# Layer 0's cross attention: scores and band mask over four quadrants, moved ahead of the attended values, with the residual between the two units on VectorE

## The chip, the core and the metric

The kernel runs on one core of one Trainium2 chip. The metric is the device time of one execution in microseconds (us); the result of a version is the median over its runs. The engines are TensorE (PE in the rows; PEld are its weight loads), VectorE (DVE), ScalarE (ACT), GpSimd (POOL) and SyncE (SP). Each engine works through its own instruction queue in order; engines wait for each other by semaphores.

## The reference, cut to what matters

The program is a decoder of two layers. After each sublayer the input is added back and normalised. Only the second sublayer, the cross attention of layer 0, is touched:

```python
q = heads(query @ Wq.T + bq)      # 32 sequences of 128 tokens, D = 256, H = 16 heads of HD = 16
k = heads(key @ Wk.T + bk)        # key = value = the context, 32 x 128 x 256
v = heads(value @ Wv.T + bv)
scores = einsum('bhqd,bhkd->bhqk', q, k) / sqrt(16)
local  = abs(i[:, None] - i[None, :]) <= 64            # a band: 128 queries x 128 keys
attn   = softmax(where(local, scores, -inf), axis=-1)
ctx    = einsum('bhqk,bhkd->bhqd', attn, v)
x      = layernorm(x + (ctx.reshape(B, S, 256) @ Wo.T + bo))
```

## The kernel before

`l0_xattn` handles one sequence of 128 tokens as one tile: 32 tiles, numbered `n`, in 8 groups of 4. The 16 heads of a tile are two units `u` of 8 heads. In a unit, `q` picks a half of the unit and `c` a half of the model dimension; the four combinations (`u`, `q`) are four quarters of 32 partitions of the projected queries and keys, and each quarter's scores have a PSUM bank of their own.

A list called `walk` sets the order on every engine: for step `s` it calls each entry `(lag, count, f)` as `f(s - lag)`. So the entries' order is the order of the engine's queue inside a step, and the lag says which tile is handled. Before the change, step `s` holds:

* **TensorE**: `score(s)` (matmuls of 32 rows, line 973, then the band mask as matmuls of a 64-row identity with `bandb`, line 978; once for each unit), `transpose_e(s-2)` (four blocks `j` of four transposes, line 992; blocks 0 and 1 are unit 0, blocks 2 and 3 are unit 1), one part of the projections of a group to come (a group's four parts, `transposes`, `project_q`, `project_k`, `project_v`, lines 934 to 959, fall on four steps in a row, and the last group's on steps 24 to 27), `apply(s-2)` (attended values, line 1001), `multiply(s-3)` (output projection, line 1013).
* **VectorE**: `shift(s)` for both units (maximum, line 1091, and subtraction, line 1094), `sums(s-1)` (row sums, line 1099, and reciprocal `ri`, line 1102), `bias_v` once in a group (line 1110), `residual(s-3)` (lines 1119 to 1126).
* **GpSimd**: `scale_e(s-1)`, which multiplies the exponentials of both units by `ri` (line 882), and at some steps `bias_x` or `roots`.
* **ScalarE**: `copy_et(s-2)` (line 1060), a part's bias or copy, `exponentials(s)` (line 1054), `copy_ot(s-2)` (line 1065), `normalise(s-8)`.

The waits that matter here: `shift` waits for `scored`; `scale_e(n)` waits for `inverted`, which `sums(n)` raises; `transpose_e(n)` waits for `e_scaled`, which `scale_e(n)` raises once for each unit; `residual(n)` waits for `multiplied`. A scored unit's bank is written again once `shifted` says that it was read.

The band mask is made ahead of step 0: GpSimd cuts it (lines 859 to 865), ScalarE copies it to bf16 (line 1027) before it copies the first transposed inputs (`copy_xt`, line 1033). No score is computed before it is there.

Of the kernel before, what the change touches and what calls it, by code (L numbers as in the profile page):

```python
# [8 lines left out]
BF16 = mybir.dt.bfloat16  # L9
I32 = mybir.dt.int32  # L10
U32 = mybir.dt.uint32
ALU = mybir.AluOpType
ACT = mybir.ActivationFunctionType
AX = mybir.AxisListType

P = 128
# [33 lines left out]
def item_done(eng, sem, n, inc=1):  # L50

    eng.wait_ge(sem, (n + 1) * inc)
# [722 lines left out]
def l0_xattn(nc, x_in, ctx4, bv, bo, ah, kv, x_out):  # L775
# [4 lines left out]
    with ExitStack() as stack:  # L780
        kit = Kit(nc, stack, "l0x")
        ident, identb = ah.ident, ah.identb
        band = kit.sb("band", [P, 4, P])
        bandb = kit.sb("bandb", [P, 4, P], BF16)
        w_q, w_k, w_v, w_o = ah.l0_w
        b_q, b_k, par = ah.l0_b_q, ah.l0_b_k, ah.l0_par
        b_v, b_o = kit.sb("b_v", [P, D]), kit.sb("b_o", [P, D])
# [68 lines left out]
        with nc.Block() as block:  # L856
            @block.gpsimd
            def _(pool):
                pool.memset(band[:, :, :], 0.0).then_inc(band_set, 1)
                pool.wait_ge(band_set, 1)  # L860

                pool.affine_select(out=band[:, :, :], in_=band[:, :, :], compare_op=ALU.is_ge, fill=-1e30, base=64,
                                   pattern=[[0, 4], [-1, P]], channel_multiplier=1).then_inc(band_cut, 1)
                pool.wait_ge(band_cut, 1)
                pool.affine_select(out=band[:, :, :], in_=band[:, :, :], compare_op=ALU.is_ge, fill=-1e30, base=64,
                                   pattern=[[0, 4], [1, P]], channel_multiplier=-1).then_inc(band_cut, 1)
                pool.memset(half[:, :], -0.5).then_inc(set_, 1)
                pool.memset(neg[:, :], -1.0).then_inc(set_, 1)
                pool.memset(eps[:, :], LN_EPS).then_inc(set_, 1)
                pool.wait_ge(set_, 3)  # L870
                pool.wait_ge(biases_loaded, 2 * 16)

                def bias_x(g):
                    x_ready(pool, g)
                    slot_free(pool, residual_done, g, 2, G)
                    pool.tensor_tensor(xb[:, g % 2, :, :], x_group(g), b_o[:, :].unsqueeze(1).to_broadcast([P, G, D]),
                                       ALU.add).then_inc(x_biased, 1)

                def scale_e(n):
                    item_done(pool, inverted, n)  # L880
                    for u in range(2):
                        pool.tensor_tensor(e[:, n % 2, u, :, :], e[:, n % 2, u, :, :], spread(ri[:, n % 2, u, :], P),  # L882
                                           ALU.mult).then_inc(e_scaled, 1)
                count = [0]

                def roots(g):
                    item_done(pool, mv_done, g, G)
                    slot_free(pool, normed, g, 2, G)
                    pool.tensor_tensor(ln[:, g % 2, 2, :], mv[:, g % 2, :, 1], eps[:, :], ALU.add).then_inc(ln_step, 1)
                    pool.wait_ge(ln_step, 3 * g + 1)  # L890
                    pool.tensor_tensor(ln[:, g % 2, 0, :], ln[:, g % 2, 2, :], half[:, :], ALU.pow).then_inc(ln_step, 1)
                    pool.wait_ge(ln_step, 3 * g + 2)
                    pool.tensor_tensor(ln[:, g % 2, 3, :], mv[:, g % 2, :, 0], ln[:, g % 2, 0, :], ALU.mult).then_inc(ln_step, 1)
                    pool.wait_ge(ln_step, 3 * g + 3)
                    pool.tensor_tensor(ln[:, g % 2, 1, :], ln[:, g % 2, 3, :], neg[:, :], ALU.mult).then_inc(ln_done, 1)
                walk([(1, TILES, scale_e), at_part(5, bias_x), (G + 3, TILES, lambda n: roots(n // G) if n % G == 0 else None)])
# [31 lines left out]
            def _(pe):  # L928
# [34 lines left out]
                def score(n):  # L963
                    g, t = n // G, n % G
                    if n == 0:
                        pe.wait_ge(band_ready, 1)
                    item_done(pe, k_biased, g, 4)
                    for u in range(2):
                        slot_free(pe, shifted, 2 * n + u, 2)
                        for c in range(2):  # L970
                            for q in range(2):
                                at = slice(32 * (2 * u + q), 32 * (2 * u + q) + 32)
                                pe.matmul(ps_s[u][:, q, 2 * c:2 * c + 2, :], qt[at, g % 2, c, t * P:(t + 1) * P],
                                          kt[at, g % 2, c, :, t * P:(t + 1) * P], start=c == 0, stop=False)
                        for q in range(2):
                            for lo in range(2):
                                rows64, keys64 = slice(64 * lo, 64 * lo + 64), slice(64 - 64 * lo, 128 - 64 * lo)
                                last = pe.matmul(ps_s[u][rows64, q, :, keys64], identb[rows64, rows64], bandb[rows64, :, keys64],
                                                 start=False, stop=True)
                        last.then_inc(scored, 1)  # L980

                def transpose_e(n):
                    for j in range(4):
                        item_done(pe, e_scaled, 2 * n + j // 2)
                        if j == 0:
                            slot_free(pe, ot_copied, n, 1)
                        elif j == 1:
                            slot_free(pe, residual_done, n, 2)
                        else:
                            pe.wait_ge(et_copied, 4 * n + j - 1)  # L990
                        for i in range(4):
                            last = pe.transpose(ps_e[j % 2][:, i, :], e[:, n % 2, j // 2, 4 * (j % 2) + i, :], ident[:, :])  # L992
                        last.then_inc(e_transposed, 1)
# [23 lines left out]
                def early(n):  # L1017
                    if n == 0:
                        pe.wait_ge(v_biased, TILES)
                    kv.make(pe, n, n + 1)  # L1020
                walk([(0, TILES, score), (2, TILES, transpose_e), at_part(0, transposes), at_part(1, project_q), at_part(2, project_k),
                      at_part(3, project_v), (2, TILES, apply), (3, TILES, multiply), (TILES + 1, L0X_LAST, early)])

            @block.scalar
            def _(act):
                act.wait_ge(band_cut, 2)
                act.activation(bandb[:, :, :], band[:, :, :], ACT.Copy).then_inc(band_ready, 1)

                def copy_xt(g):
# [17 lines left out]
                            act.activation(kt[:, g % 2, c, odd, :], ps_p[c][:, :], ACT.Identity, bias=b_kp[:, odd, c:c + 1],  # L1047
                                           scale=par[:, odd:odd + 1]).then_inc(k_biased, 1)

                def exponentials(n):  # L1050
                    slot_free(act, e_transposed, n, 2, 4)
                    for u in range(2):
                        item_done(act, shifted, 2 * n + u)
                        act.activation(e[:, n % 2, u, :, :], sx[:, u, :, :], ACT.Exp, scale=HD ** -0.5).then_inc(exped, 1)

                def copy_et(n):
                    slot_free(act, applied, n, 1)
                    for j in range(4):
                        item_done(act, e_transposed, 4 * n + j)
                        act.activation(et[:, j, :, :], ps_e[j % 2][:, :, :], ACT.Copy).then_inc(et_copied, 1)  # L1060

# [5 lines left out]
                def normalise(n):  # L1067
# [2 lines left out]
                    slot_free(act, stored[g % 2], g // 2, 1, 16)  # L1070
                    act.activation(y[:, g % 2, t, :], r[:, g % 2, t, :], ACT.Identity, scale=ln[:, g % 2, 0, t:t + 1],
                                   bias=ln[:, g % 2, 1, t:t + 1]).then_inc(normed, 1)
                walk([(2, TILES, copy_et), at_part(0, copy_xt), at_part(1, bias_q), at_part(2, bias_k), (0, TILES, exponentials),
                      (2, TILES, copy_ot), (8, TILES, normalise), (TILES + 1, 2, lambda n: kv.keep(act, n, n + 1)),
                      (TILES + 5, L0X_LAST - 2, lambda n: kv.keep(act, n + 2, n + 3))])

            @block.vector
            def _(dve):
# [3 lines left out]
                    ins = dve.tensor_scalar(b_kp[:, odd, :], b_k[:, :], par[:, odd:odd + 1], None, ALU.mult)  # L1082
                ins.then_inc(bkp_done, 1)

                def shift(n):
                    for u in range(2):
                        i = 2 * n + u
                        item_done(dve, scored, i)
                        scores = ps_s[u][:, :, :, :].rearrange("p q h k -> p (q h) k")
                        slot_free(dve, shifted, i, 2)  # L1090
                        dve.tensor_reduce(top[:, u, :], scores, AX.X, ALU.max).then_inc(maxed, 1)
                        item_done(dve, maxed, i)
                        slot_free(dve, exped, i, 2)
                        dve.tensor_tensor(sx[:, u, :, :], scores, spread(top[:, u, :], P), ALU.subtract).then_inc(shifted, 1)

                def sums(n):
                    item_done(dve, exped, n, 2)
# [16 lines left out]
                def residual(n):  # L1114
# [9 lines left out]
                    item_done(dve, stats_done, n)  # L1124
                    slot_free(dve, ln_done, g, 2)
                    dve.bn_aggr(mv[:, g % 2, t, :], stats[:, n % 2, :]).then_inc(mv_done, 1)
                walk([(0, TILES, shift), (1, TILES, sums), at_part(3, bias_v), (3, TILES, residual)])
        kit.clear_semaphores()

# [1856 lines left out]
```

## Time and profile before

| what | value |
|---|---|
| median of 3 runs | 2455.33 us (2452.11 to 2456.83) |
| the profiled execution | 2453.8 us, span 2452.1 us |
| granted TensorE clock over the span | 0.971 |
| busy share of the span: PE, DVE, ACT, POOL | 92%, 55%, 45%, 35% |
| the stage that is changed | from about 446 to 800 us of the span |

### The profile page before, as it was taken

To read this page: it belongs to the slowest core of one execution; us is meant where nothing else is said; L and a number is where in the kernel's file an instruction comes from. 1 tells how busy PE (TensorE), PEld (TensorE's weight loads), DVE (VectorE), ACT (ScalarE), POOL (GpSimd) and SP (SyncE) were. 2 spreads that over 40 slices of the span, in tenths; PEclk is the share of its full clock that TensorE was granted. 3 is DMA by queue.
4 is the path that set the end of the run, shared out by engine and by line. 5 is a ranking of instruction groups with operands and counts; after the bars stand their busy time and mean duration, and the time that the engine had idled before them with its cause. 6 is when DMAs were issued, how large, how long until landed. Compare 5 with 4: busy or idle time off the path is not lost. (4 is left out here: it accounts for less than half of the span.)

```text
span 2452.1 us, 44501 instructions
## 1 busy us (share of the span) xinstructions
PE 2262.6 (92%) x17122; PEld 1768.8 (72%) x17122; DVE 1347.3 (55%) x2517; ACT 1100.5 (45%) x1872; POOL 849.8 (35%) x873
## 2 busy tenths in 40 slices
PE   7999998799998899999999799999995999999993
PEld 5777776466666566757776688888884888888893
DVE  6888888488887680015545567888885111111113
ACT  3666666456565564543334255555552111111113
POOL 3555454244444582000101234455444122222221
PEclk8999999899999999999999899999997999999997
DMA  5435554100110679480211323333332856666665
GB/s 144 113 90 129 137 128 115 61 27 27 53 53 19 214 254 295 149 262 4 69 50 37 112 90 106 104 104 109 104 121 76 293 174 191 193 174 183 194 203 148
DMA packets 204609, 313.21 MB, mean 128 GB/s; under 512 B 63473, under 2 KB 183153, under 8 KB 191089
## 3 DMA queue, kind: packets, MB, share of 16 engines
q1 hardware_dynamic: 184336, 255.25, 33.6%
q0 software_dynamic: 13440, 17.90, 4.1%
q10 hardware_dynamic: 6624, 37.23, 3.9%
q8 instruction: 138, 2.26, 0.4%
q14 instruction: 71, 0.57, 0.1%
HBM read 188.88 MB, written 121.45 MB: 127 GB/s over the span
## 5 line engine op out<-in xcount | busy, mean ns | idle before, releaser
L2748 ACT ACTIVATE dec_area<-me_ps_h 128x512 f32<-128x512 f32 (+1 forms) x160 | 88.7, 554 | 423.8 <-PE me_ps_h L2726 423.8
L2789 DVE TENSOR_SCALAR me_yo<-me_ps_y,moe_xg 128x256 f32<-128x256 f32 x72 | 34.8, 484 | 429.2 <-PE me_ps_y L2736 391.3
L2664 POOL DMA_INDIRECT xo<-me_yo,me_row x72 | 112.7, 1565 | 410.7 <-DVE me_yo L2789 350.2
L2726 PE MATMUL me_ps_h<-me_xt,me_w 128*128 128x256 f32 (+1 forms) x1056 | 210.1, 357 | 0.0
L2736 PE MATMUL me_ps_y<-me_w,dec_area 128*128 128x256 f32 x944 | 209.2, 379 | 0.7 <-DVE me_yo L2789 0.7
L2199 POOL TENSOR_TENSOR l1x_e<-l1x_e,l1x_ri 128x1024 f32<-128x1024 f32 x64 | 121.7, 1901 | 240.8 <-DVE l1x_ri L2459 240.8
L2736 PEld LDWEIGHTS me_ps_y<-me_w,dec_area 128*128 128x128 f32 x944 | 179.0, 190 | 24.8 <-issue 1.1
L2726 PEld LDWEIGHTS me_ps_h<-me_xt,me_w 128*128 128x128 f32 x1056 | 181.9, 191 | 20.0
L882 POOL TENSOR_TENSOR l0x_e<-l0x_e,l0x_ri 128x1024 f32<-128x1024 f32 x64 | 120.0, 1896 | 186.9 <-DVE l0x_ri L1102 186.9
L2298 PE MATMUL l1x_ps_p<-l1x_xct,dec_area 128*128 128x256 f32 x512 | 126.4, 392 | 1.0 <-ACT l1x_xct L2384 1.0
L2336 PE MATMUL l1x_ps_o<-dec_area,l1x_ot 128*128 128x256 f32 x512 | 120.4, 389 | 1.4 <-ACT l1x_ot L2407 1.4
L2397 ACT ACTIVATE l1x_e<-l1x_sx 128x1024 f32<-128x1024 f32 x64 | 67.4, 1054 | 116.0 <-DVE l1x_sx L2450 115.9
L1060 ACT ACTIVATE l0x_et<-l0x_ps_e 128x512 f32<-128x512 f32 x128 | 70.0, 595 | 91.6 <-PE l0x_ps_e L992 91.2
L2336 PEld LDWEIGHTS l1x_ps_o<-dec_area,l1x_ot 128*128 128x128 f32 x512 | 96.1, 193 | 15.5 <-ACT l1x_ot L2407 1.7
L587 DVE SCALAR_TENSOR_TENSOR l0ah_c<-l0ah_f,l0ah_ps_s 128x1024 f32<-128x1024 f32 x64 | 77.2, 1206 | 52.6 <-ACT l0ah_f L751 52.6
L2298 PEld LDWEIGHTS l1x_ps_p<-l1x_xct,dec_area 128*128 128x128 f32 x512 | 95.5, 196 | 14.5 <-ACT l1x_xct L2384 1.6
L2456 DVE TENSOR_REDUCE l1x_rs<-l1x_e 128x8 f32<-128x1024 f32 x64 | 78.0, 1219 | 49.0 <-ACT l1x_e L2397 48.5
L2447 DVE TENSOR_REDUCE l1x_top<-l1x_ps_s 128x8 f32<-128x1024 f32 x64 | 77.6, 1212 | 47.9 <-PE l1x_ps_s L2309 47.5
L763 ACT ACTIVATE l0ah_et<-l0ah_ps_e 128x512 f32<-128x512 f32 x128 | 76.4, 597 | 58.8 <-PE l0ah_ps_e L701 57.9
L494 POOL TENSOR_SCALAR_AFFINE_SELECT l0ah_e<-l0ah_e 128x1024 f32<-128x1024 f32 x64 | 69.9, 1092 | 91.9 <-ACT l0ah_e L757 90.8
L751 ACT ACTIVATE l0ah_f<-l0ah_ps_s 128x1024 f32<-128x1024 f32 x64 | 65.5, 1024 | 59.5 <-PE l0ah_ps_s L681 56.6
L490 POOL TENSOR_TENSOR l0ah_wt<-l0ah_c,l0ah_fs 128x1024 f32<-128x1024 f32 x32 | 60.7, 1897 | 88.5 <-DVE l0ah_fs L614 88.5
(414 smaller groups left out, 5335.5 us busy)
## 6 DMA issues: line engine op xcount, KB each, us to landing
me_w<-in_w SPq DMA_DIRECT2D x33, 2048.0 KB, 9.5
xs<-dec_zero SPq DMA_DIRECT2D x31, 1032.0 KB
k<-kv_kt ACTq DMA_DIRECT2D x16, 1024.0 KB, 5.5
v<-kv_va ACTq DMA_DIRECT2D x16, 1024.0 KB, 5.2
l1x_kt<-k SPq DMA_DIRECT2D x16, 1024.0 KB, 5.1
l1x_va<-v SPq DMA_DIRECT2D x16, 1024.0 KB, 5.8
moe_w_first<-in_w SPq DMA_DIRECT2D x7, 2048.0 KB, 9.8
moe_xg<-xs SPq DMA_DIRECT2D x32, 258.0 KB, 2.8
```

The costliest lines, as they stand in the source:

```text
L587: dve.scalar_tensor_tensor(out=c[:, n % 2, u, :, :].rearrange("p (r g) k -> p r g k", g=2), in0=f[:, u, :, :].rearrange("p (r g) k -> p r ...
L763: act.activation(et[:, j // 2, 4 * (j % 2):4 * (j % 2) + 4, :], ps_e[j % 2][:, :, :], ACT.Copy).then_inc(et_copied, 1)
L882: pool.tensor_tensor(e[:, n % 2, u, :, :], e[:, n % 2, u, :, :], spread(ri[:, n % 2, u, :], P), ALU.mult).then_inc(e_scaled, 1)
L2199: pool.tensor_tensor(e[:, n % 2, u, :, :], e[:, n % 2, u, :, :], spread(ri[:, n % 2, u, :], P), ALU.mult).then_inc(e_scaled, 1)
L2298: last = pe.matmul(ps_p[i % 2][:, c * GP:(c + 1) * GP], w_q[:, k, at], xct[:, k, :], start=k == 0, stop=k == 1)
L2336: last = pe.matmul(ps_o[:, 0:2, :].rearrange("p a b -> p (a b)"), ot[:, c, :], w_o[:, c, :], start=c == 0, stop=c == C - 1)
L2447: dve.tensor_reduce(top[:, u, :], scores, AX.X, ALU.max).then_inc(maxed, 1)
L2456: dve.tensor_reduce(rs[:, n % 2, u, :], e[:, n % 2, u, :, :], AX.X, ALU.add).then_inc(summed, 1)
L2664: pool.indirect_dma_start(token_rows, bass.IndirectOffsetOnAxis(row[:, j % 2, q:q + 1], 0), yo[:, j % 2, q, :], None, compute_op=ALU.add). ...
L2726: last = pe.matmul(ps_h[i % HB][:, f % 2, 0:P * size(j)], weights(j)[:, FFN * c + f * P:FFN * c + f * P + P], xt[:, j % 2, c, 0:P * size(j ...
L2736: last = pe.matmul(ps_y[q][:, 0:D], h[:, j % 2, f, q * P:(q + 1) * P], weights(j)[:, W2 + D * f:W2 + D * f + D], start=f == 0, stop=f == F ...
L2748: act.activation(h[:, j % 2, 2 * i:2 * i + 2, 0:P * size(j)], ps_h[i % HB][:, :, 0:P * size(j)], ACT.Gelu).then_inc(gelued, 1)
```

## The change

Four things change in `l0_xattn`.

1. **Scores.** Both units are scored together: for each `c`, all four quarters follow one another. The scores therefore wait until both units of the tile before are shifted.
2. **Band mask.** For `q` = 1 the mask is fed from the other 64 partitions, through a second mask `swapb`, so that the four matmuls of a unit use the four 64 x 64 quadrants of the array. `swapb` is made ahead of step 0: one more memset and two more cuts on GpSimd, two more copies on ScalarE.
3. **TensorE's order in a step** becomes: blocks 0 and 1 of `transpose_e(s-2)`, the projection's part, blocks 2 and 3 of `transpose_e(s-2)`, `score(s)`, `apply(s-2)`, `multiply(s-3)`.
4. **ScalarE and VectorE** follow: ScalarE takes the exponentials of unit 1 one step later, as `exponentials(s-1, 1)`; VectorE's step becomes `bias_v`, unit 0 of `shift(s)`, `residual(s-3)`, unit 1 of `shift(s)`, `sums(s-1)`.

The core of the diff (the new masks, `shift` and `copy_et` by parts are cut to what says most):

```diff
                 pool.memset(band[:, :, :], 0.0).then_inc(band_set, 1)
-                pool.wait_ge(band_set, 1)
+                pool.memset(swap[:, :, :, :], 0.0).then_inc(band_set, 1)
+                pool.wait_ge(band_set, 2)
...
+                pool.affine_select(out=swap[:, 0, :, :], in_=swap[:, 0, :, :], compare_op=ALU.is_ge, fill=-1e30, base=0,
+                                   pattern=[[0, 4], [1, P]], channel_multiplier=-1).then_inc(band_cut, 1)
+                pool.affine_select(out=swap[:, 1, :, :], in_=swap[:, 1, :, :], compare_op=ALU.is_ge, fill=-1e30, base=0,
+                                   pattern=[[0, 4], [-1, P]], channel_multiplier=1).then_inc(band_cut, 1)
...
                     if n == 0:
-                        pe.wait_ge(band_ready, 1)
+                        pe.wait_ge(band_ready, 2)
                     item_done(pe, k_biased, g, 4)
+                    slot_free(pe, shifted, 2 * n + 1, 2)
+                    for c in range(2):
+                        for quarter in range(4):
+                            u, q = quarter // 2, quarter % 2
+                            at = slice(32 * quarter, 32 * quarter + 32)
+                            pe.matmul(ps_s[u][:, q, 2 * c:2 * c + 2, :], qt[at, g % 2, c, t * P:(t + 1) * P],
+                                      kt[at, g % 2, c, :, t * P:(t + 1) * P], start=c == 0, stop=False)
                     for u in range(2):
-                        slot_free(pe, shifted, 2 * n + u, 2)
-                        for c in range(2):
-                            for q in range(2):
-                                at = slice(32 * (2 * u + q), 32 * (2 * u + q) + 32)
-                                pe.matmul(ps_s[u][:, q, 2 * c:2 * c + 2, :], ...
                         for q in range(2):
                             for lo in range(2):
                                 rows64, keys64 = slice(64 * lo, 64 * lo + 64), slice(64 - 64 * lo, 128 - 64 * lo)
-                                last = pe.matmul(ps_s[u][rows64, q, :, keys64], identb[rows64, rows64], bandb[rows64, :, keys64],
+                                held = slice(64 * (lo ^ q), 64 * (lo ^ q) + 64)
+                                last = pe.matmul(ps_s[u][rows64, q, :, keys64], identb[held, held], (swapb if q else bandb)[held, :, keys64],
                                                  start=False, stop=True)
                         last.then_inc(scored, 1)
...
-                walk([(0, TILES, score), (2, TILES, transpose_e), at_part(0, transposes), at_part(1, project_q), at_part(2, project_k),
-                      at_part(3, project_v), (2, TILES, apply), (3, TILES, multiply), (TILES + 1, L0X_LAST, early)])
+                walk([(2, TILES, lambda n: transpose_e(n, (0, 1))), at_part(0, transposes), at_part(1, project_q), at_part(2, project_k),
+                      at_part(3, project_v), (2, TILES, lambda n: transpose_e(n, (2, 3))), (0, TILES, score), (2, TILES, apply), (3, TILES, multiply),
+                      (TILES + 1, L0X_LAST, early)])
...
-                act.wait_ge(band_cut, 2)
+                act.wait_ge(band_cut, 4)
+                act.activation(swapb[0:64, :, :], swap[0:64, 0, :, :], ACT.Copy)
+                act.activation(swapb[64:128, :, :], swap[64:128, 1, :, :], ACT.Copy).then_inc(band_ready, 1)
                 act.activation(bandb[:, :, :], band[:, :, :], ACT.Copy).then_inc(band_ready, 1)
...
-                walk([(2, TILES, copy_et), at_part(0, copy_xt), at_part(1, bias_q), at_part(2, bias_k), (0, TILES, exponentials),
-                      (2, TILES, copy_ot), (8, TILES, normalise), (TILES + 1, 2, lambda n: kv.keep(act, n, n + 1)),
+                walk([(2, TILES, lambda n: copy_et(n, (0, 1))), at_part(0, copy_xt), at_part(1, bias_q), at_part(2, bias_k),
+                      (2, TILES, lambda n: copy_et(n, (2, 3))), (1, TILES, lambda n: exponentials(n, 1)), (2, TILES, copy_ot),
+                      (0, TILES, lambda n: exponentials(n, 0)), (8, TILES, normalise), (TILES + 1, 2, lambda n: kv.keep(act, n, n + 1)),
...
-                walk([(0, TILES, shift), (1, TILES, sums), at_part(3, bias_v), (3, TILES, residual)])
+                walk([at_part(3, bias_v), (0, TILES, lambda n: shift(n, 0)), (3, TILES, residual), (0, TILES, lambda n: shift(n, 1)), (1, TILES, sums)])
```

## Rows read from the trace of the kernel before

**Rows 1.** Busy time by engine, steady stretch; columns: us, then PE, PEld, DVE, ACT, POOL, granted clock, DMA share, GB/s.
```profile
600.00:650.00 50.00, 47.83 (x418) 31.19 (x415) 41.48 (x46) 29.77 (x50) 22.98 (x16) 1.00 0.11 33
```
**Rows 2.** Timeline of TensorE, one step; columns: start us, busy us, what.
```profile
609.55 1.13 PE L973 MATMUL l0x_ps_s<-l0x_kt,l0x_qt 32*128 32x256 f32 x8
610.61 0.41 PE L978 MATMUL l0x_ps_s<-l0x_bandb,dec_identb 64*64 64x256 bf16 x4
...
612.35 1.09 PE L992 MATMUL l0x_ps_e<-dec_ident,l0x_e 128*128 128x128 f32 x8
613.84 1.12 PE L992 MATMUL l0x_ps_e<-dec_ident,l0x_e 128*128 128x128 f32 x8 [0.40 <-ACT l0x_et L1060]
614.79 3.62 PE L959 MATMUL l0x_ps_p<-dec_area,l0x_cxt 128*128 128x256 f32 x16
618.34 1.08 PE L1001 MATMUL l0x_ps_e<-l0x_et,l0x_va 128*32 128x128 f32 x32
...
620.41 1.13 PE L973 MATMUL l0x_ps_s<-l0x_kt,l0x_qt 32*128 32x256 f32 x8
```
**Rows 3.** Timeline of VectorE, one step in which it never idles.
```profile
621.92 1.22 DVE L1091 TENSOR_REDUCE l0x_top<-l0x_ps_s 128x8 f32<-128x1024 f32 x1 [0.30 <-PE l0x_ps_s L978]
...
626.71 2.27 DVE L1099 TENSOR_REDUCE l0x_rs<-l0x_e 128x16 f32<-128x2048 f32 x1
629.02 0.25 DVE L1102 RECIPROCAL l0x_ri<-l0x_rs 128x16 f32<-128x16 f32 x1
...
630.21 1.23 DVE L1091 TENSOR_REDUCE l0x_top<-l0x_ps_s 128x8 f32<-128x1024 f32 x1
```
**Rows 4.** Timelines of VectorE, GpSimd and TensorE: reciprocal, scaling, transposes after the last score.
```profile
776.84 0.25 DVE L1102 RECIPROCAL l0x_ri<-l0x_rs 128x16 f32<-128x16 f32 x1
...
777.17 3.75 POOL L882 TENSOR_TENSOR l0x_e<-l0x_e,l0x_ri 128x1024 f32<-128x1024 f32 x2 [4.45 <-DVE l0x_ri L1102]
...
779.12 3.53 PE L992 MATMUL l0x_ps_e<-dec_ident,l0x_e 128*128 128x128 f32 x16 [2.38 <-POOL l0x_e L882]
```
**Rows 5.** Timeline of TensorE: the scores of tile 1 and of tile 31 begin.
```profile
467.00 1.13 PE L973 MATMUL l0x_ps_s<-l0x_kt,l0x_qt 32*128 32x256 f32 x8 [0.25 <-DVE l0x_sx L1094]
...
768.23 1.13 PE L973 MATMUL l0x_ps_s<-l0x_kt,l0x_qt 32*128 32x256 f32 x8
```
**Rows 6.** Timeline of TensorE in the self attention before: scores over four groups of 32 rows.
```profile
200.99 0.61 PE L678 MATMUL l0ah_ps_s<-l0a_guardb,dec_identb 128*128 128x256 bf16 x4
201.53 0.73 PE L681 MATMUL l0ah_ps_s<-l0ah_ops 32*128 32x128 f32 x16
202.19 0.64 PE L714 MATMUL l0ah_ps_e<-l0ah_et,l0ah_va 128*32 128x128 f32 x16
```
**Rows 7.** Timeline of TensorE where it restarts after idling, then busy time and clock from there.
```profile
446.19 1.94 PE L934 MATMUL l0x_ps_p<-dec_ident,dec_area 128*128 128x128 f32 x8 [8.12 <-PEq L85]
...
804.10 9.76 PE L1269 MATMUL ffn_ps_kv<-kv_w_kv,kv_ct 128*128 128x512 f32 x16 [5.38 <-PEq L85]
...
1076.07 3.52 PE L1977 MATMUL ma_ps_t<-dec_ident,mw_xin 128*128 128x128 f32 x16 [5.33 <-PEq L85]
...
446.19:454.50 8.31, 6.42 (x14) 3.47 (x15) 1.06 (x3) 2.29 (x4) 1.86 (x6) 0.50 0.65 221
...
804.10:809.40 5.30, 5.30 (x7) 2.20 (x8) 0.00 (x0) 0.60 (x1) 5.30 (x1) 0.50 0.69 188
...
1076.07:1079.10 3.03, 3.03 (x14) 2.66 (x15) 1.62 (x9) 1.19 (x2) 0.09 (x2) 0.50 0.41 109
```
**Rows 8.** Timelines of GpSimd and ScalarE ahead of step 0.
```profile
446.82 0.63 POOL L862 TENSOR_SCALAR_AFFINE_SELECT l0x_band<-l0x_band 128x512 f32<-128x512 f32 x1
...
448.80 1.06 ACT L1033 ACTIVATE l0x_xt<-l0x_ps_p 128x512 f32<-128x512 f32 x2
```
**Rows 9.** Timelines of TensorE and VectorE in the last steps.
```profile
785.32 0.60 PE L992 MATMUL l0x_ps_e<-dec_ident,l0x_e 128*128 128x128 f32 x4
...
785.52 0.42 DVE L1119 TENSOR_TENSOR l0x_r<-l0x_ps_e,l0x_xb 128x256 f32<-128x256 f32 x1 [5.00 <-PE l0x_ps_e L1013]
```

More of the change, by code:

```diff
@@ L784, in l0_xattn @@
         bandb = kit.sb("bandb", [P, 4, P], BF16)
+        swap = kit.sb("swap", [P, 2, 4, P])
+        swapb = kit.sb("swapb", [P, 4, P], BF16)
         w_q, w_k, w_v, w_o = ah.l0_w
@@ L965, in score @@
                     if n == 0:
-                        pe.wait_ge(band_ready, 1)
+                        pe.wait_ge(band_ready, 2)
                     item_done(pe, k_biased, g, 4)
-                    for u in range(2):
-                        slot_free(pe, shifted, 2 * n + u, 2)
-                        for c in range(2):
-                            for q in range(2):
-                                at = slice(32 * (2 * u + q), 32 * (2 * u + q) + 32)
-                                pe.matmul(ps_s[u][:, q, 2 * c:2 * c + 2, :], qt[at, g % 2, c, t * P:(t + 1) * P],
-                                          kt[at, g % 2, c, :, t * P:(t + 1) * P], start=c == 0, stop=False)
+                    slot_free(pe, shifted, 2 * n + 1, 2)
[5 more added lines that the diff above has]
+                                      kt[at, g % 2, c, :, t * P:(t + 1) * P], start=c == 0, stop=False)
+                    for u in range(2):
                         for q in range(2):
@@ L977, in score, with transpose_e @@
                                 rows64, keys64 = slice(64 * lo, 64 * lo + 64), slice(64 - 64 * lo, 128 - 64 * lo)
-                                last = pe.matmul(ps_s[u][rows64, q, :, keys64], identb[rows64, rows64], bandb[rows64, :, keys64],
+                                held = slice(64 * (lo ^ q), 64 * (lo ^ q) + 64)
+                                last = pe.matmul(ps_s[u][rows64, q, :, keys64], identb[held, held], (swapb if q else bandb)[held, :, keys64],
                                                  start=False, stop=True)
                         last.then_inc(scored, 1)
-                def transpose_e(n):
-                    for j in range(4):
+                def transpose_e(n, parts):
+                    for j in parts:
                         item_done(pe, e_scaled, 2 * n + j // 2)
@@ L1048, in bias_k, with exponentials, copy_et @@
                                            scale=par[:, odd:odd + 1]).then_inc(k_biased, 1)
-                def exponentials(n):
+                def exponentials(n, u):
                     slot_free(act, e_transposed, n, 2, 4)
[L1052 to L1056, printed above, removed]
+                    item_done(act, shifted, 2 * n + u)
+                    act.activation(e[:, n % 2, u, :, :], sx[:, u, :, :], ACT.Exp, scale=HD ** -0.5).then_inc(exped, 1)
+                def copy_et(n, parts):
                     slot_free(act, applied, n, 1)
-                    for j in range(4):
+                    for j in parts:
                         item_done(act, e_transposed, 4 * n + j)
@@ L1083, in _, with shift @@
                 ins.then_inc(bkp_done, 1)
[L1085 to L1094, printed above, removed]
+                def shift(n, u):
+                    i = 2 * n + u
+                    item_done(dve, scored, i)
+                    scores = ps_s[u][:, :, :, :].rearrange("p q h k -> p (q h) k")
+                    slot_free(dve, shifted, i, 2)
+                    dve.tensor_reduce(top[:, u, :], scores, AX.X, ALU.max).then_inc(maxed, 1)
+                    item_done(dve, maxed, i)
+                    slot_free(dve, exped, i, 2)
+                    dve.tensor_tensor(sx[:, u, :, :], scores, spread(top[:, u, :], P), ALU.subtract).then_inc(shifted, 1)
                 def sums(n):
```

## The prediction

> **What bounds the kernel now.** I read the busy time of the steady stretch first. There TensorE works for 47.83 of 50 us and VectorE for 41.48, at full clock [rows 1]. So TensorE sets the pace of this stage and VectorE follows closely. Then I read the timeline of TensorE for one step. From one tile's first score to the next it is 609.55 to 620.41, 10.86 us, in this order: scores of both units 2.80 us (609.55 to 612.35), transposes 2.44 us with one wait of 0.40, a projection part 3.55 us, attended values and output projection together 2.07 us [rows 2]. Over the stage the scores of tile 1 begin at 467.00 and those of tile 31 at 768.23 [rows 5]: 30 steps in 301.2 us, 10.04 us each.
>
> Third, VectorE. In a step without idle time it needs 8.29 us from one first maximum to the next (621.92 to 630.21), and its reciprocal lies inside, at 629.02 [rows 3]. Last, the hand-over that I hold to be decisive: after the last score, where nothing else covers it, the reciprocal ends at 777.09 (776.84 + 0.25), GpSimd scales both units from 777.17 for 3.75 us, and the transposes start at 779.12, once the first unit is scaled [rows 4]. So 2.03 us pass from reciprocal to first transpose, and the second unit is there at 780.92, 1.85 us after the first and 3.9 us after the reciprocal, with a hand-over of some 0.05.
>
> Why does this not show in the steady step? The scores of step s+1 stand ahead of the transposes in TensorE's queue. While GpSimd scales tile s-1, TensorE scores tile s+1, and VectorE gets its next input. One way round through sums, scaling and transposes back to a score spans two steps.
>
> **The change, part by part.**
>
> *Scores and mask.* For one unit, eight records of 32 rows by 256 columns now take 1.06 us (609.55 to 610.61), and its four mask matmuls the rest of 1.40 us, half of the 2.80, so 0.34 [rows 2]; afterwards sixteen follow one another over four quarters. If four quarters run at once, they take the same 1.06 us, and the mask for both units some 0.34: 1.40 us in place of 2.80. If only two run at once the scores take 2.12 us. The nearest rows are those of the self attention, where sixteen records over four groups of 32 rows, 128 columns wide, take 0.66 us (201.53 to 202.19) [rows 6]. The full-height transposes of the same width take 2.44 - 0.40 = 2.04 us for sixteen records [rows 2]. A ratio of three, with the change of tile shape inside the 0.66, says four at once; I take 1.40 us. From the first score to VectorE's first maximum it is now 620.41 to 621.92, 1.51 us [rows 2, 3]; the first unit's four mask matmuls come one round earlier if they share the quadrants, so 1.4 us.
>
> Whether the mask's quadrants really run together is the second question. Four bf16 matmuls of 256 columns at full size take 0.54 us (200.99 to 201.53) [rows 6], the four of 64 rows here 0.34 us with the change of shape inside [rows 2], so at least two of them overlap, and they do so on one bank. I let the four of a unit run at once. If they ran one after another, the first unit would come some 0.4 us later, in 30 steps 12 us.
>
> The Trainium skill, "TensorEngine Tiling (Array Packing)", section "Gotcha 1: PSUM Pressure", says that different row tiles cannot access the same PSUM bank at the same time, and here the two halves of a `q` are such tiles on one bank. By that rule the sum would be 2727 us in place of 2715; the 0.34 us against 0.54 speaks against it in this trace.
>
> *TensorE's order.* This is the term that decides. Scores of step s+1 now stand behind all four transposes of tile s-1 and behind the projection's part. These transposes wait for GpSimd's scaling of tile s-1, which waits for `sums(s-1)`, and VectorE does those last in step s, behind unit 1's shift of tile s. VectorE's next work, `shift(s+1, 0)`, waits for the score. So one way round now fits in one step, and nothing in it overlaps:
>
> - VectorE: both shifts, residual and sums, 8.29 us [rows 3], to the reciprocal's end;
> - reciprocal to first transpose, 2.03 us [rows 4];
> - TensorE: two blocks of transposes 0.95 us (613.84 to 614.79), the part, two blocks 0.95 us and a change of shape, 1.0 us [rows 2];
> - first score to first maximum, 1.4 us.
>
> The part is 3.55 us for a projection (I take the values' for all three), 1.0 us for the group's transposes of inputs (eight records of 128 x 128, as in a pair of blocks), or nothing. A projection step takes 8.3 + 2.03 + 0.95 + 3.55 + 1.0 + 1.4 = 17.2 us. One with input transposes takes 14.7 us. One without a part waits for the second unit: 8.3 + 3.9 + 1.0 + 1.4 = 14.6 us. Steps 2 to 31 hold 20, 6 and 4 of these (the last part is that of step 27): 344 + 88 + 58 = 490 us against 301.2 now. **This costs 189 us.**
>
> Is something in the loop later still? ScalarE copies the last two blocks while TensorE scores, so the attended values start when the scores end; with the output projection they need 2.07 us [rows 2], which ends about when unit 0 is shifted. So the residual between the units waits for little. After the output projection TensorE has nothing: it idles while VectorE does residual, unit 1 and sums and GpSimd scales the first unit, 11.7 - 3.5 = 8.2 us in every step.
>
> *TensorE's clock.* Here the idle time has a price. In this trace TensorE idled 5.33, 5.38 and 8.12 us, and every time the granted clock stood at 0.50 (1.2 GHz) when it began again; it stayed there for 3.03, 5.30 and 8.31 us [rows 7]. At 1.2 GHz a matmul streams half as fast: sixteen transpose records take 3.53 us in place of 2.04 [rows 4, 2]. In the first two cases TensorE then worked without a pause, as it will here from transposes to scores; their mean is 4.2 us, and half of that is lost, 2.1 us in each of 26 steps. In the four steps without a part 0.95 us of it falls into the wait for the second unit, 1.15 us each. **Together 59 us.** The bounds are nothing, if the clock stays up, and 8.3 us of half clock, which is 4.15 x 26 + 3.2 x 4 = 121 us.
>
> *Ahead of step 0.* A cut takes 0.63 us on GpSimd, a pair of ScalarE's copies of the same width 1.06 [rows 8]. One memset of twice the width (at the cut's price 1.3 us, an upper bound; no row here shows it), two cuts (1.3) and two copies (1.1) come before `copy_xt`, now at 448.80, and on TensorE the first projections wait for that: 3.7 us, say 4. The new buffers carry no transfer.
>
> *Behind step 31.* VectorE now does `residual(29)` ahead of `sums(31)`. That residual is at 785.52, while the transposes of tile 31 already begin at 785.32 [rows 9]. They will have to wait for residual (629.27 to 630.21, 0.9 us), sums (626.71 to 629.27, 2.6) [rows 3] and scaling (2.0) after it, and the step before is 0.9 us later for its own residual: some 7 us, and 2 us for half a clock after that idle time. I take 9.
>
> *At no cost.* ScalarE's unit 1 a step later is behind the 11 us in which only VectorE, GpSimd and the transposes work; the extra wait of the scores for both units is met long before the transposes are. Without that cover it would be one shift, 2.4 us (half of 621.92 to 626.71 [rows 3]).
>
> The sum against the profiled execution: 2453.8 + 189 + 59 + 4 + 9 = 2714.8, so **2715 us**. That execution lies 1.5 us below the median of before; I leave the difference out.
>
> **The rivals.**
>
> *The loop does not close (faster).* Mechanism: the first transposes find unit 0 scaled when the output projection ends. Then TensorE's step is shorter by 1.40 us, 8.64, which is still above VectorE's 8.29, and 30 steps save 42 us: 2453.8 - 42 + 13 = 2425. It decides at a reciprocal that ends 2 us before the output projection does. For it: TensorE is nearly full now and would be relieved. Against it: the sums stand behind both shifts in VectorE's queue, and the reciprocal so comes about 6 us after the output projection.
>
> *The loop closes and the clock stays up.* No half clock in the steps: 2715 - 59 = 2656. For it: after 5.33 us of idling the half clock lasted 3.03 us only. Against it: all three restarts after more than 5 us were at half clock [rows 7].
>
> *The loop closes and costs more.* Half clock as long as 8.3 us: 2715 + 62 = 2777. Or only two quarters at once: 1.06 us more in 30 steps, 2747.
>
> *The mask's quadrants one after another.* 2727, as above; for it only that no row shows four of them together.
>
> *The relief is given back exactly.* That time stands within 0.2% would need the loop to cost as much as the scores save, 1.4 us in a step; the shortest wait in it, 2.03 us, is already longer, and the part comes on top.
>
> **How the numbers follow.** The forecast's case has 0.67, the clock that stays up 0.12, the dearer loop 0.13, the mask in turn 0.03; the open loop has 0.03 and no difference 0.02. A difference below about 0.2%, 5 us, could not be told from none here. Slower by more than that: 0.67 + 0.12 + 0.13 + 0.03 = 0.95. The range takes in both clock bounds, 2656 and 2777, with some microseconds for the small terms: 2650 to 2785.
>
> **What would show it.** Right: TensorE's transposes (line 992 in before) idle each step with GpSimd's scaling as releaser; VectorE's first maximum waits 6 to 9 us for the scores in every step; step lengths near 19 us with a projection and 16 to 17 without; the granted clock falls to 0.50 in each step and returns; sixteen score records in about 1.1 us at full clock. The step of the loop is wrong if VectorE goes from the reciprocal to the next maximum within 1 to 2 us; the clock term is wrong if the granted clock of the stage stays above 0.95. The prediction as a whole is wrong if the reciprocal of a step comes before the output projection of that step.

## The result, and the profile after

The changed kernel takes 2723.98 us (median of 4 runs, 2721.19 to 2730.67) against 2454.51 us for the kernel before; the ratio is 1.1102, with a 95% interval of [1.1077, 1.1127]. It is slower by 269 us. The forecast was 2715 us. The profiled execution took 2730.67 us, span 2728.6 us.

First the busy time by engine in a stretch of the changed stage (columns as in [rows 1]), and under it five pieces of it: TensorE's idle time, what follows at half clock and at full clock, and the same two of the next step.

```profile
600.00:750.00 150.00, 84.17 (x688) 59.40 (x688) 68.41 (x81) 51.92 (x80) 37.78 (x26) 0.75 0.05 15
651.62:659.65 8.03, 0.01 (x1) 0.00 (x0) 5.87 (x8) 1.55 (x2) 1.95 (x2) 0.75 0.00 0
659.65:662.50 2.85, 2.85 (x11) 2.67 (x12) 0.00 (x0) 1.20 (x2) 1.80 (x1) 0.50 0.00 0
662.50:669.94 7.44, 7.44 (x82) 5.65 (x81) 3.61 (x6) 2.42 (x4) 0.00 (x0) 1.00 0.01 2
678.19:683.00 4.81, 4.81 (x23) 4.81 (x24) 0.00 (x0) 2.58 (x5) 3.38 (x5) 0.50 0.00 0
683.00:686.84 3.84, 3.83 (x63) 2.46 (x61) 2.10 (x2) 2.31 (x4) 0.00 (x0) 1.00 0.00 0
```

TensorE worked 47.83 of 50 us before [rows 1]; now it works 84 of 150. No engine is near full any more, which is the mark of a chain in which each waits for the next. TensorE's timeline for one step shows the wait and its releaser:

```profile
659.65 1.97 PE L1001 MATMUL l0x_ps_e<-dec_ident,l0x_e 128*128 128x128 f32 x8 [8.03 <-POOL l0x_e L889]
661.41 4.16 PE L966 MATMUL l0x_ps_p<-dec_area,l0x_cxt 128*128 128x256 f32 x16
665.41 1.04 PE L1001 MATMUL l0x_ps_e<-dec_ident,l0x_e 128*128 128x128 f32 x8
666.38 1.15 PE L980 MATMUL l0x_ps_s<-l0x_kt,l0x_qt 32*128 32x256 f32 x16
667.45 0.30 PE L987 MATMUL l0x_ps_s<-l0x_bandb,dec_identb 64*64 64x256 bf16 x2
667.46 0.30 PE L987 MATMUL l0x_ps_s<-l0x_swapb,dec_identb 64*64 64x256 bf16 x2
667.59 0.27 PE L987 MATMUL l0x_ps_s<-l0x_bandb,dec_identb 64*64 64x256 bf16 x2
667.59 0.27 PE L987 MATMUL l0x_ps_s<-l0x_swapb,dec_identb 64*64 64x256 bf16 x2
667.79 1.08 PE L1010 MATMUL l0x_ps_e<-l0x_et,l0x_va 128*32 128x128 f32 x32
...
678.19 1.97 PE L1001 MATMUL l0x_ps_e<-dec_ident,l0x_e 128*128 128x128 f32 x8 [8.25 <-POOL l0x_e L889]
...
683.28 1.15 PE L980 MATMUL l0x_ps_s<-l0x_kt,l0x_qt 32*128 32x256 f32 x16
```

VectorE and GpSimd in the same step:

```profile
667.81 1.23 DVE L1102 TENSOR_REDUCE l0x_top<-l0x_ps_s 128x8 f32<-128x1024 f32 x1 [1.44 <-PE l0x_ps_s L987]
...
670.21 0.41 DVE L1130 TENSOR_TENSOR l0x_r<-l0x_ps_e,l0x_xb 128x256 f32<-128x256 f32 x1
...
675.90 0.25 DVE L1113 RECIPROCAL l0x_ri<-l0x_rs 128x16 f32<-128x16 f32 x1
684.71 1.23 DVE L1102 TENSOR_REDUCE l0x_top<-l0x_ps_s 128x8 f32<-128x1024 f32 x1 [8.55 <-PE l0x_ps_s L987]
...
676.24 3.75 POOL L889 TENSOR_TENSOR l0x_e<-l0x_e,l0x_ri 128x1024 f32<-128x1024 f32 x2 [14.78 <-DVE l0x_ri L1113]
```

One way round can be read off: maximum at 667.81, reciprocal done at 676.15 (675.90 + 0.25; 8.34 us), first transpose at 678.19 (2.04 us later, 2.03 in [rows 4]), transposes, part and transposes to the scores at 683.28 (5.09 us), next maximum at 684.71 (1.43 us). The residual at 670.21 waits for nothing, and VectorE waits 8.55 us from reciprocal to maximum.

Where the 277 us between the two profiled executions (2730.67 and 2453.8) lie, by the starts of scores in the timelines:

```profile
451.67 1.94 PE L941 MATMUL l0x_ps_p<-dec_ident,dec_area 128*128 128x128 f32 x8 [8.14 <-PEq L85]
...
458.86 3.75 PE L950 MATMUL l0x_ps_p<-l0x_xt,dec_area 128*128 128x512 f32 x4 [5.25 <-ACT l0x_xt L1045]
...
472.22 0.60 PE L941 MATMUL l0x_ps_p<-dec_ident,l0x_x 128*128 128x128 f32 x4
...
480.27 1.15 PE L980 MATMUL l0x_ps_s<-l0x_kt,l0x_qt 32*128 32x256 f32 x16 [1.33 <-DVE l0x_sx L1105]
...
1031.48 1.15 PE L980 MATMUL l0x_ps_s<-l0x_kt,l0x_qt 32*128 32x256 f32 x16
...
1057.42 3.90 PE L1001 MATMUL l0x_ps_e<-dec_ident,l0x_e 128*128 128x128 f32 x16 [5.64 <-POOL l0x_e L889]
```

| stretch | before | after | more | forecast |
|---|---|---|---|---|
| scores of tile 1 to scores of tile 31 [rows 5] | 301.2 | 551.2 | 250.0 | 248 (189 + 59) |
| stage's start to the first scores (446.19 to 462.86; 451.67 to 473.82) | 16.7 | 22.2 | 5.5 | 4 |
| scores of tile 31 to the next stage's first matmul (804.10 [rows 7]; 1078.85) | 35.9 | 47.4 | 11.5 | 9 |
| all the rest | | | 9.9 | 0 |

Of the rest 5.5 us lie ahead of the stage (451.67 against 446.19), in code that is the same in both, and 2.3 between the scores of tile 0 and of tile 1 (6.45 us in place of 4.14), where the scores now wait for both units' subtraction (1.33 us at 480.27). The profiled execution is the slowest of the four, 6.7 us above their median.

### The profile page after: what moved, and what is told of

It reads as the page before. It is cut to its first block and busy times, and to the rows that moved or that the text cites. A ratio compares the mean times of both kernels' runs of the same rounds, so it can differ in the third digit from the quotient of the medians.

```text
span 2728.6 us, 44569 instructions
## 1 busy us (share of the span) xinstructions
PE 2293.2 (84%) x17122; PEld 1803.4 (66%) x17122; DVE 1348.8 (49%) x2517; ACT 1113.3 (41%) x1874; POOL 853.1 (31%) x876
## 5 line engine op out<-in xcount | busy, mean ns | idle before, releaser
L1001 PE MATMUL l0x_ps_e<-dec_ident,l0x_e 128*128 128x128 f32 x512 | 105.2, 374 | 261.1 <-POOL l0x_e L889 261.1
L1001 PEld LDWEIGHTS l0x_ps_e<-dec_ident,l0x_e 128*128 128x128 f32 x512 | 87.8, 197 | 284.0 <-POOL l0x_e L889 276.0
L1102 DVE TENSOR_REDUCE l0x_top<-l0x_ps_s 128x8 f32<-128x1024 f32 x64 | 77.8, 1215 | 244.6 <-PE l0x_ps_s L987 244.6
L2347 PEld LDWEIGHTS l1x_ps_o<-dec_area,l1x_ot 128*128 128x128 f32 x512 | 94.7, 190 | 15.2 <-ACT l1x_ot L2418 1.7
```

The costliest lines, as they stand in the source:

```text
L2347: last = pe.matmul(ps_o[:, 0:2, :].rearrange("p a b -> p (a b)"), ot[:, c, :], w_o[:, c, :], start=c == 0, stop=c == C - 1)
```

## The experiments

The theory: the reordering closes a loop within one step, score, shift, sums, scaling, transposes, score, and TensorE's idle time in it lowers its clock. The main rival: scoring both units together, which waits for both shifts, is what costs.

**Orders alone.** Scores and mask as before, the three new orders kept:

```diff
                     for u in range(2):
+                        slot_free(pe, shifted, 2 * n + u, 2)
+                        for c in range(2):
+                            for q in range(2):
...
-                                last = pe.matmul(..., identb[held, held], (swapb if q else bandb)[held, :, keys64],
+                                last = pe.matmul(..., identb[rows64, rows64], bandb[rows64, :, keys64],
```

> The scores unit by unit and the band mask as before; the three orders of the changed kernel (TensorE, ScalarE, VectorE) kept. Loop theory: the orders carry the whole price. The first unit is scored as early as in the changed kernel, but the attended values and the output projection come 1.4 us later, so that the residual between the units comes some 1.3 us late: 30 steps of 1.4 us more than the changed kernel's 2724, less 5 us ahead of step 0: about 2760. Rival (the price lies in scoring both units together, which waits for both shifts): about 2454.

It took 2744.33 us, ratio 1.1182 [1.1163, 1.1201]. The orders carry the whole price, and more: the rival falls. The dearer scores cost 20 us more than the changed kernel, not 36. VectorE's timeline shows why the dearer scores cost anything, the residual now waiting for the output projection:

```profile
685.00 0.42 DVE L1119 TENSOR_TENSOR l0x_r<-l0x_ps_e,l0x_xb 128x256 f32<-128x256 f32 x1 [0.98 <-PE l0x_ps_e L1013]
```

I expected this wait to be 1.3 us.

**Scores alone.** Scores and mask as changed, the three lists of before:

```diff
-                walk([(2, TILES, lambda n: transpose_e(n, (0, 1))), at_part(0, transposes), ...
+                walk([(0, TILES, score), (2, TILES, lambda n: transpose_e(n, (0, 1, 2, 3))), at_part(0, transposes), ...
...
-                walk([at_part(3, bias_v), (0, TILES, lambda n: shift(n, 0)), (3, TILES, residual), (0, TILES, lambda n: shift(n, 1)), (1, TILES, sums)])
+                walk([(0, TILES, lambda n: shift(n, 0)), (0, TILES, lambda n: shift(n, 1)), (1, TILES, sums), at_part(3, bias_v), (3, TILES, residual)])
```

> The scores and the mask over four quadrants as changed; the three orders as before. Loop theory: nothing closes, TensorE's step is 1.4 us shorter, 30 steps 42 us, and 5 us are lost ahead of step 0: about 2417. Rival (joint scores wait for both shifts): about 2700. Second rival (quadrants do not run at once): about 2455.

2455.81 us, ratio 1.0003 [0.9993, 1.0014]: no loss, but no gain either. My 42 us were wrong. TensorE's timeline, and busy time and clock from its restart:

```profile
634.39 1.15 PE L980 MATMUL l0x_ps_s<-l0x_kt,l0x_qt 32*128 32x256 f32 x16
...
638.30 3.89 PE L1001 MATMUL l0x_ps_e<-dec_ident,l0x_e 128*128 128x128 f32 x16 [2.42 <-POOL l0x_e L889]
...
648.84 1.15 PE L980 MATMUL l0x_ps_s<-l0x_kt,l0x_qt 32*128 32x256 f32 x16
```
```profile
638.30:644.50 6.20, 6.20 (x19) 4.26 (x20) 6.08 (x6) 2.39 (x4) 1.80 (x1) 0.50 0.01 3
```

The scores are shorter: steps with the key and value projections take 9.5 and 9.8 us in place of 10.9, and the one with input transposes 6.9 in place of 8.3. That is less than VectorE's 8.29 [rows 3]. So the next step's transposes wait 2.42 us for the scaling, and 6.2 us at half clock follow: that step takes 14.45 us (634.39 to 648.84) in place of 11.0, and 12.9 to 15.2 us in the six groups that have such a step. Most of the saving is given back in one step of four. From tile 1 to tile 31, 296.6 us in place of 301.2, 4.6 us are left of it, and 5.3 us more go ahead of tile 1's scores: 3.0 up to the first scores, 2.3 for the wait for both units.

**Scores first on TensorE alone.** The changed kernel with one entry moved:

```diff
-                walk([(2, TILES, lambda n: transpose_e(n, (0, 1))), ..., (0, TILES, score), (2, TILES, apply), ...
+                walk([(0, TILES, score), (2, TILES, lambda n: transpose_e(n, (0, 1))), ..., (2, TILES, apply), ...
```

> The changed kernel with the scores back at the head of TensorE's step, nothing else. If TensorE's order alone closes the loop: 2420 to 2460. If the residual between VectorE's two units closes a second one (score, transposes, part, attended values, output projection, residual, unit 1's shift, next score), a projection step is 15.7 us at full clock, one without 13: 30 steps 445 us in place of 551, and with the half clock up to 505: 2610 to 2680.

2696.85 us, ratio 1.099 [1.0972, 1.1009]. Undoing the order that I had named as the decisive one gives back 27 of 269 us. The second loop is there, and TensorE's timeline names it: the scores wait for unit 1's subtraction, which stands behind the residual, and the transposes then wait for the scaling all the same.

```profile
652.36 1.13 PE L1022 MATMUL l0x_ps_e<-dec_area,l0x_ot 128*128 128x256 f32 x4
657.16 1.44 PE L980 MATMUL l0x_ps_s<-l0x_kt,l0x_qt 32*128 32x256 f32 x16 [3.67 <-DVE l0x_sx L1105]
...
661.52 1.97 PE L1001 MATMUL l0x_ps_e<-dec_ident,l0x_e 128*128 128x128 f32 x8 [2.35 <-POOL l0x_e L889]
```

The time is 17 us above the upper end that I expected. The range allowed for half clock as in the changed kernel; here scores run at half clock too (0.50 from 672.50 to 675.20 us, behind the pause of 3.67). How much of the 17 us this is was not separated: from 600 to 750 us the granted clock was 0.75, as in the changed kernel.

**Residual last on VectorE alone.** The rest as changed:

```diff
-                walk([..., (0, TILES, lambda n: shift(n, 0)), (3, TILES, residual), (0, TILES, lambda n: shift(n, 1)), (1, TILES, sums)])
+                walk([..., (0, TILES, lambda n: shift(n, 0)), (0, TILES, lambda n: shift(n, 1)), (1, TILES, sums), (3, TILES, residual)])
```

> The changed kernel with the residual behind the sums on VectorE, nothing else. Loop theory: the residual's 0.94 us leave the loop, 28 us in 30 steps, and the last steps no longer hold the last sums behind a residual, 7 us: about 2689. Rival (the residual stands in a pause that VectorE has anyway): 2724.

2683.54 us, ratio 1.0937 [1.0918, 1.0956]: 40 us less than the changed kernel, 35 expected. The residual's 0.94 us do lie in the loop; the waits that it could have hidden in are at the other end of VectorE's step.

**Both moves.** ScalarE's order as changed:

```diff
-                walk([(2, TILES, lambda n: transpose_e(n, (0, 1))), ..., (0, TILES, score), (2, TILES, apply), ...
+                walk([(0, TILES, score), (2, TILES, lambda n: transpose_e(n, (0, 1))), ..., (2, TILES, apply), ...
...
-                walk([..., (3, TILES, residual), (0, TILES, lambda n: shift(n, 1)), (1, TILES, sums)])
+                walk([..., (0, TILES, lambda n: shift(n, 1)), (1, TILES, sums), (3, TILES, residual)])
```

> The changed kernel with the scores back at the head of TensorE's step and the residual behind the sums; ScalarE's order stays as changed. If TensorE and VectorE hold all the loops: 2420 to 2460. If ScalarE's exponentials of unit 1, behind the copies of the transposes, close a third one (score, transposes, part, copies, exponentials of the tile before, subtraction of unit 1, next score): 13.3 us for a projection step, 10.8 for the others, 374 us in 30 steps in place of 551, with the half clock up to 420: 2540 to 2590.

2593.84 us, ratio 1.0569 [1.0544, 1.0594], 4 us above the range expected for a third loop and 134 above the one for none. The third loop is there too. VectorE's and ScalarE's timelines show unit 1's subtraction waiting 7.25 us for exponentials that stand behind the copies of the transposes:

```profile
670.59 1.08 ACT L1071 ACTIVATE l0x_et<-l0x_ps_e 128x512 f32<-128x512 f32 x2
671.55 1.07 ACT L1065 ACTIVATE l0x_e<-l0x_sx 128x1024 f32<-128x1024 f32 x1
...
672.72 1.23 DVE L1105 TENSOR_TENSOR l0x_sx<-l0x_ps_s,l0x_top 128x1024 f32<-128x1024 f32 x1 [7.25 <-ACT l0x_e L1065]
```

**No idle time on TensorE.** The changed kernel with matmuls that nobody reads in the pause:

```diff
+                def fill(n):
+                    item_done(pe, ot_copied, n)
+                    for i in range(32):
+                        pe.matmul(ps_e[0][:, :, :].rearrange("p a b -> p (a b)"), identb[:, :], bandb[:, :, :].rearrange("p a b -> p (a b)"),
+                                  start=True, stop=True)
...
+                      (2, TILES - 2, fill), (TILES + 1, L0X_LAST, early)])
```

> The changed kernel with 32 more matmuls of 512 bf16 columns on TensorE behind the output projection, in steps 2 to 31, which nobody reads (some 7 us of the 8.2 that it idles). Clock term: the granted clock of the stage stays at 1.00 and each step is 2.2 us shorter, 66 us: about 2658. Rival (the half clock is hidden by other waits): 2724; the matmuls get in the way: above 2724.

2659.92 us, ratio 1.0836 [1.0812, 1.0861]. 64 us come back by doing more work. Busy time and clock, and TensorE's timeline:

```profile
600.00:750.00 150.00, 137.41 (x1057) 80.49 (x1066) 76.77 (x89) 56.49 (x90) 41.95 (x29) 1.00 0.07 22
```
```profile
654.23 1.15 PE L980 MATMUL l0x_ps_s<-l0x_kt,l0x_qt 32*128 32x256 f32 x16
...
657.84 6.85 PE L1029 MATMUL l0x_ps_e<-l0x_bandb,dec_identb 128*128 128x512 bf16 x31
666.04 1.09 PE L1001 MATMUL l0x_ps_e<-dec_ident,l0x_e 128*128 128x128 f32 x8 [1.35 <-POOL l0x_e L889]
...
671.37 1.15 PE L980 MATMUL l0x_ps_s<-l0x_kt,l0x_qt 32*128 32x256 f32 x16
```

From tile 1 to tile 31 the scores are 492.9 us apart, in place of 551.2. At a clock of 1.00 a step with the query projection takes 17.14 us (654.23 to 671.37), and one with input transposes 14.69: the loop at full clock, without its clock term. In the changed kernel the four steps of a group (query, key and value projection, input transposes) take 19.57, 20.02, 18.60 and 16.90 us, here 17.14, 17.15, 17.23 and 14.69.

**Three variants of the scores alone.** They ask what the new scores are worth when no loop closes. First, the masks copied behind the first inputs:

```diff
-                act.wait_ge(band_cut, 4)
-                act.activation(swapb[0:64, :, :], swap[0:64, 0, :, :], ACT.Copy)
...
+                      at_part(0, copy_xt), at_part(0, masks), at_part(1, bias_q), ...
```

> Scores and mask as changed, orders as before, and ScalarE copies the masks behind the first group's transposed inputs in place of ahead of them. The first projection no longer waits for the masks: 5 to 6 us less than with the masks ahead, about 2411. Rival (the first scores wait for the masks all the same): no difference.

2452.29 us, ratio 0.999 [0.9976, 1.0005]: 3.5 us less than with the masks ahead, less than the 5 to 6 expected and inside the noise, since the two intervals overlap. (The 2411 and 2420 expected of this run and the next rest on the same 42 us as above and missed with it.) The traces do show the masks' price: the first scores come 15.3 us after the stage's first matmul, with the masks ahead 19.7. Second, the old mask on two quadrants, without `swapb`:

```diff
-                                last = pe.matmul(..., identb[held, held], (swapb if q else bandb)[held, :, keys64],
+                                last = pe.matmul(..., identb[rows64, rows64], bandb[rows64, :, keys64],
```

> Both units scored together, the mask on two quadrants as before (no second mask), orders as before. If the four quadrants run at once, the mask takes two rounds of 0.13 us more in each step, 8 us, and 5 us are saved ahead of step 0: about 2420, 3 more than with quadrants. Rival (different row tiles of one bank in turn): the quadrants bring nothing, 5 us less than with quadrants: 2412.

2456.03 us, ratio 0.9999 [0.9985, 1.0013]: as with four quadrants, so the time does not tell the two apart. The timelines do. In the changed kernel two `bandb` and two `swapb` matmuls start within 10 ns at 667.45 and 667.46, and the next four 0.14 us later: eight over four quadrants take 0.34 us (667.45 to 667.79). In this run eight over two quadrants take 0.56 us:

```profile
602.12 0.62 PE L979 MATMUL l0x_ps_s<-l0x_bandb,dec_identb 64*64 64x256 bf16 x8
602.68 1.09 PE L993 MATMUL l0x_ps_e<-dec_ident,l0x_e 128*128 128x128 f32 x8
```

Third, the query projection ahead of the transposes in its step, on top of the late masks, so that it covers the wait of 2.42 us:

```diff
-                walk([(0, TILES, score), (2, TILES, lambda n: transpose_e(n, (0, 1, 2, 3))), at_part(0, transposes), at_part(1, project_q), ...
+                walk([(0, TILES, score), at_part(1, project_q), (2, TILES, lambda n: transpose_e(n, (0, 1, 2, 3))), at_part(0, transposes), ...
```

> Scores and mask as changed, masks copied late, orders as before, and the query projection moved ahead of the transposes in its step. With the scores alone, the step behind the short one (6.9 us) waits 2.42 us for GpSimd's scaling and then runs on at half clock, 13.3 to 14.5 us. If this wait eats the 1.4 us a step that the scores save, the projection covers it, and the step falls to about 10: 3.6 us less in each of 7 groups, 25 us: about 2427. Rival (VectorE sets the pace anyway, and the wait moves to another step): 2452.

2437.24 us, ratio 0.9933 [0.9917, 0.995]: faster than both kernels, 0.7% faster than the one before. Clock and timeline:

```profile
600.00:720.00 120.00, 109.36 (x1120) 74.81 (x1112) 110.06 (x129) 79.62 (x130) 58.74 (x41) 1.00 0.16 54
```
```profile
616.38 1.15 PE L980 MATMUL l0x_ps_s<-l0x_kt,l0x_qt 32*128 32x256 f32 x16
...
617.80 3.70 PE L950 MATMUL l0x_ps_p<-l0x_xt,dec_area 128*128 128x512 f32 x8
621.34 1.04 PE L1001 MATMUL l0x_ps_e<-dec_ident,l0x_e 128*128 128x128 f32 x8
...
626.65 1.15 PE L980 MATMUL l0x_ps_s<-l0x_kt,l0x_qt 32*128 32x256 f32 x16
```

The step falls to 10.3 us and the clock stays at 1.00. 15 of the 25 us came: the key projection's step grew from 9.5 to 10.2 us, and the first of the seven groups had no long step to shorten (7.57 us without this move, 7.73 with it). The control, the same move in the kernel before:

> The kernel before with the query projection ahead of the transposes in its step, nothing else: a control. There that step waits 0.4 us only, and the attended values would wait some 0.7 us for ScalarE's last copies with no projection between: no gain, 2455 to 2460. Rival (the order alone is worth it, without the scores together): below 2445.

2458.11 us, ratio 1.0012 [1.0001, 1.0023]: the order alone brings nothing. It is worth something only where the shorter scores have made a wait for it to cover.

## Why the prediction was right

*The loop* (189 us forecast). Right in mechanism and size. Without the half clock the steps are 17.14 to 17.23 us with a projection and 14.69 with input transposes, against 17.2 and 14.7 forecast, and the thirty steps of the filled pause take 191.7 us more than before (492.9 against 301.2). Its pieces stand in the timeline: 8.34, 2.04, 5.09 and 1.43 us. What I did not say is that two more loops lie behind it. I named TensorE's order as the term that decides; with the scores back at the head the kernel still takes 2697 us, and with the residual moved as well 2594. So the term was sized rightly, but undoing it alone would not have saved the kernel. The second and the third loop are read from the waits in those two runs; no run changes VectorE's or ScalarE's list alone, so that each would close a loop by itself is not shown.

*The clock* (59 us, 2.1 us a step). Right: 2.43, 2.87, 1.37 and 2.21 us in the four steps of a group (the differences above), 2.2 us in the mean, 58.3 us over the thirty steps (551.2 - 492.9) and 64 us for the kernel. The half clock lasted 2.85 and 4.81 us after the restarts shown; the two rows that the price was taken from had 3.03 and 5.30 [rows 7]. That the mean came out so closely is in part luck: single steps lost 1.37 to 2.87 us, and the rows allowed anything from nothing to 4.15.

*Scores and mask* (1.40 us). Right: scores from 666.38 to 667.45, 1.07 us for sixteen records, and the mask to 667.79, together 1.41, in the step at full clock. All four quarters run at once. The Trainium skill's rule of "TensorEngine Tiling (Array Packing)", section "Gotcha 1: PSUM Pressure", would have the two row tiles of one bank take turns; the four starts within 10 ns do not agree with that for tiles that write different partitions of the bank.

*Ahead of step 0* and *behind step 31* (4 and 9 us): 5.5 and 11.5 us, both somewhat dearer. The masks delay the first copy nearly as worked out (458.86 - 451.67 = 7.2 us to the first projection, against 450.01 - 446.19 = 3.8 before: 3.4 us for 3.7). What I had left out is that step 0's input transposes now stand ahead of the first scores (1.6 us, 472.22 to 473.82; before they came behind them); another 0.6 us is a longer half clock in the first projection. Behind step 31 the transposes of tile 31 wait 5.64 us for the residual, the sums and the scaling.

*The rivals.* The mask's quadrants one after another, 2727 us, lie nearer to the measured 2724 than the forecast does; it is the starts within 10 ns that rule them out, not the time. The open loop, 2425 us, was ruled out; and its price was wrong too. It supposed that TensorE's 1.40 us a step would reach the end if no loop closed. The scores alone gave nothing, since VectorE's 8.29 us, which the short step falls below, and the half clock in the step behind it take it back. The clock that stays up (2656) is what the filled pause shows, 2660. Why the key projection's step grew in the fastest version is only read from its timeline, not tried.

## What to carry to other kernels

Before an entry is moved in a list that fills in-order queues, follow one round of the dependences and count over how many steps it reaches. Here the scores of the next tile had stood ahead of the transposes that wait for the scaling; put behind them, they made a round that had spanned two steps fit into one, and durations that used to overlap add up. Look at every engine's list, since several loops can close together and the longest hides the others; undoing one shows the next. A saving on the fullest engine is worth only what the second fullest leaves, step by step and not in the mean; where it becomes a pause, give the pause work that is due anyway.

## What the runs showed of the hardware that I had not expected

A pause of 2.42 us on TensorE was followed by 6.2 us at half clock (scores alone, 638.30 to 644.50), while a pause of 1.35 us in each step left it at 1.00 (filled pause). I could have seen the first in the kernel before: after 2.38 us of idling sixteen transpose records took 3.53 us in place of 2.04 [rows 4, 2], at a granted clock of 0.50 from 779.12 to 782.10, and yet I gave the half clock no price where no loop closes. In the filled kernel more matmuls made the program 64 us shorter.
